# Key scratch in device memory: one copy per slot of a head, two loads per unit instead of six

## The reference, cut to what matters

```python
k = jnp.einsum('btd,dnh->btnh', source_input, wk)        # layer 0; layer 1 is alike
logits = jnp.einsum('btnh,bfnh->bnft', k, q * HEAD_DIM ** (-0.5))
attn = jnp.einsum('bnft,btnh->bfnh', softmax(logits), v)
x = x + jnp.einsum('bfnh,nhd->bfd', attn, wo)
```

## Time and profile before

| | |
|---|---|
| median of 3 runs | 303.28 us |
| the traced execution itself | 301.85 us, span 299.8 us |
| PE, DVE, ACT, POOL busy | 93%, 76%, 69%, 23% of the span |
| granted TensorE clock | full (1.0) throughout |
| DMA | 27.54 MB; HBM read 20.42 MB, written 6.42 MB |
| stores of kparts | 24 of 256 KB |
| loads of kpair | 186: 62 each of 96, 64 and 32 KB |

### The profile page before, as it was taken

How to read it: one execution, slowest core, us unless ns; L and a number is a source line. 1 busy time by engine, 2 the same in 40 slices (tenths; PEclk the granted TensorE clock), 3 DMA queues, 4 the chain that set the end, 5 groups by cost and what they waited for, 6 DMA issues and landing times.

```text
span 299.8 us, 10438 instructions
## 1 busy us (share of the span) xinstructions
PE 278.4 (93%) x4414; PEld 178.8 (60%) x4418; DVE 226.8 (76%) x376; ACT 207.3 (69%) x427; POOL 68.9 (23%) x139
## 2 busy tenths in 40 slices
PE   7989899989899989889999999999889988899995
PEld 6445567656666655453656577676556655436675
DVE  5877699989799982474478999998899860744583
ACT  7864789988778978622444889999788976234350
POOL 5603475101111012510022874101010210110001
PEclk9999999999999999999999999999999999999999
DMA  7954515532222470233200026422222100000000
GB/s 249 415 203 119 157 56 174 179 119 85 63 58 81 110 275 0 107 132 104 83 1 2 3 83 223 149 81 81 61 78 65 46 2 2 2 0 2 0 2 22
DMA packets 10737, 27.54 MB, mean 92 GB/s; under 512 B 2193, under 2 KB 3313, under 8 KB 10306
## 3 DMA queue, kind: packets, MB, share of 16 engines
q1 hardware_dynamic: 10640, 26.83, 27.1%
q10 hardware_dynamic: 50, 0.03, 0.0%
HBM read 20.42 MB, written 6.42 MB: 90 GB/s over the span
## 4 chain that ended last, share of the span: by engine, by line
PE 63%; DVE 13%; SPq 7%; DMA 6%; ACT 5%; issue 4%; POOL 1%; DVEq 0%; POOLq 0%
PE bank L1160 61%; SPq L306 6%; DVE mx L913 6%; DMA kpair<-k_scratch 4%; ACT probs L605 3%; DMA ctxT_s<-in_ctxT 2%; DVE o_rec L869 1%; DVE v_all L860 1%; DVE s_neg L969 1%; DVE xn L836 1%; DVE st L817 1%; PE bank L1497 1%; PE bank L1541 0%; ACT kpair L740 0%; SPq L329 0%
## 5 line engine op out<-in xcount | busy, mean ns | idle before, releaser
L913 DVE TENSOR_REDUCE mx<-bank 128x2 f32<-128x1024 f32 x128 | 149.8, 1215 | 9.1 <-PE bank L1160 7.7
L605 ACT ACTIVATE probs<-bank 128x512 f32<-128x512 f32 x256 | 140.7, 597 | 21.4 <-PE bank L1160 17.9
L1160 PE MATMUL bank<-q_exp,kpair 64*128 64x128 bf16 x1024 | 82.4, 218 | 1.1 <-ACT q_exp L528 1.1
L1160 PE MATMUL bank<-probs,v_all 128*9 128x128 f32 x2048 | 79.9, 274 | 2.0 <-ACT probs L605 1.4
L1160 PE MATMUL bank<-kpair,q_rows 64*128 64x512 bf16 x256 | 68.0, 382 | 8.9 <-DVE mx L913 5.4
L1160 PEld LDWEIGHTS bank<-q_exp,kpair 64*128 64x128 bf16 x1024 | 55.1, 94 | 28.9 <-ACT probs L605 14.5
L1160 PEld LDWEIGHTS bank<-probs,v_all 128*9 128x9 f32 x2048 | 43.4, 90 | 18.6 <-ACT probs L605 4.8
L471 POOL CAST m_rows<-negm 128x2 bf16<-128x2 f32 x32 | 6.3, 197 | 131.1 <-DVE negm L920 131.1
L1160 PEld LDWEIGHTS bank<-kpair,q_rows 64*128 64x128 bf16 x256 | 20.9, 93 | 16.3 <-DVE mx L913 8.1
L528 ACT ACTIVATE v_all<-bank 128x512 f32<-128x512 f32 (+1 forms) x20 | 10.6, 536 | 13.7 <-PE bank L1160 13.7
L395 POOL TENSOR_TENSOR y<-ve,mhalf 128x1 f32<-128x1 f32 (+1 forms) x10 | 5.8, 580 | 53.1 <-DVE ve L823 53.1
(11 more groups left out here) (230 smaller groups left out, 349.9 us busy)
## 6 DMA issues: line engine op xcount, KB each, us to landing
k_scratch<-kparts SPq DMA_DIRECT2D x24, 256.0 KB, 3.3
kpair<-k_scratch SPq DMA_DIRECT2D x62, 96.0 KB
kpair<-k_scratch SPq DMA_DIRECT2D x62, 64.0 KB
ctxT_s<-in_ctxT SPq DMA_DIRECT2D x4, 512.0 KB, 9.0
mask_s<-in_mask SPq DMA_DIRECT2D x2, 1024.0 KB, 9.6
kpair<-k_scratch SPq DMA_DIRECT2D x62, 32.0 KB
wM<-in_packM SPq DMA_DIRECT2D x1, 1728.0 KB, 7.0
wB<-in_packB SPq DMA_DIRECT2D x1, 654.0 KB, 6.4
```

What stands on the lines that cost most here:

```text
L605: act.activation(probs[:, j % 4, :], slot_bank(l, "b", n, j), ACT.Exp).then_inc(S("slot_free"), 1)
L913: V.tensor_reduce(mx[n % 2][:, w, :], bank[:, 2 * (w % 2):2 * (w % 2) + 2, :], AX.X, ALU.max) \
L1160: return T.matmul(out_, lhsT=lhsT, rhs=rhs, start=start, stop=stop, **kw)
```

## The change

The scratch tensor holds the 6 slots of every head in place of the 3 parts. A store writes a key part into each of its slots in one transfer (source repeated); a load takes a whole head, 48 rows of 4 KB, in one transfer. The tables that place queries and first keys follow the new row order, slot first and dimension second.

```diff
-K_LOADS = 2 * PARTS
+K_LOADS = 2
+STORES = 2 * PARTS
-kscr = nc.dram_tensor("k_scratch", (2, B, PARTS, H, HD, SK), BF16, kind="Internal").ap()
+kscr = nc.dram_tensor("k_scratch", (2, B, len(SLOTS), H, HD, SK), BF16, kind="Internal").ap()
 def load_head(eng, l, p, b, u, a):
-    for kp in range(PARTS):
-        times = K_TIMES[kp]
-        row = a * HOFF + K_BASE[kp]
-        src = kscr[l, b, kp, p * 2 + a:p * 2 + a + 1, :, :].rearrange("h d t -> (h d) t")
-        src = src.unsqueeze(1).to_broadcast([HD, times, SK])
-        eng.dma_start(kpair[u][row:row + times * HD, :], src).then_inc(S(f"k_loaded{u}"), 16)
+    src = kscr[l, b, :, p * 2 + a, :, :]
+    eng.dma_start(kpair[u][a * HOFF:a * HOFF + HR, :], src).then_inc(S(f"k_loaded{u}"), 16)
 # store_k
     for kp in range(PARTS):
-        sp.dma_start(kscr[l, b, kp, :, :, t:t + SK // 2],
-                     kparts[:, kp, b * SK + t:b * SK + t + SK // 2]).then_inc(S(f"k_stored{b}"), 16)
+        first = K_BASE[kp] // HD
+        dst = kscr[l, b, first:first + K_TIMES[kp], :, :, t:t + SK // 2].rearrange("s h d t -> (h d) s t")
+        src = kparts[:, kp, b * SK + t:b * SK + t + SK // 2].unsqueeze(1)
+        sp.dma_start(dst, src.to_broadcast([P, K_TIMES[kp], SK // 2])).then_inc(S(f"k_stored{b}"), 16)
 # constants(): selq and selk
-    (h % 2) * HOFF + K_BASE[kp] + d * K_TIMES[kp] + qp
+    (h % 2) * HOFF + K_BASE[kp] + qp * HD + d
```

More of the change, by code:

```diff
@@ L337, in cross_k @@
                 if n % NP == (l == 0 and n < NP):
-                    sp.wait_ge(S(f"k_stored{n // NP}"), 16 * 2 * PARTS * (l + 1))
+                    sp.wait_ge(S(f"k_stored{n // NP}"), 16 * STORES * (l + 1))
                 if l or n >= U:
@@ L449, in split_k @@
                 if l and i == 0:
-                    pool.wait_ge(S("k_stored1"), 16 * 2 * PARTS)
+                    pool.wait_ge(S("k_stored1"), 16 * STORES)
                 pool.tensor_copy(kparts[:, 0, cols], s_sb[:, i, :]).then_inc(S("k_pool"), 1)
@@ L532, in prep_k @@
                 if l and c == 0:
-                    act.wait_ge(S("k_stored0"), 16 * 2 * PARTS)
+                    act.wait_ge(S("k_stored0"), 16 * STORES)
                 copy(kparts[:, 0, c * 512:(c + 1) * 512], bank[:, k_bank(l, c), :]).then_inc(S("k_high"), 1)
@@ L1735, in constants @@
             for d in range(HD):
-                selq[h * HD + d, h // 2 % 2, qp, (h % 2) * HOFF + K_BASE[kp] + d * K_TIMES[kp] + qp] = one
+                selq[h * HD + d, h // 2 % 2, qp, (h % 2) * HOFF + K_BASE[kp] + qp * HD + d] = one
     selk = np.zeros((4 * HD, PARTS, P), np.uint16)
@@ L1740, in constants @@
             for d in range(HD):
-                selk[h * HD + d, kp, h * HOFF + K_BASE[kp] + d * K_TIMES[kp] + qp] = one
+                selk[h * HD + d, kp, h * HOFF + K_BASE[kp] + qp * HD + d] = one
     kone = np.array([[float(r % HOFF >= HR)] for r in range(P)], np.float32)
```

## The result

The changed kernel took 311.44 us in the median (309.30 to 312.31, 4 runs) where the kernel before took 303.01 on the same chip (300.60 to 303.51, 4 runs): a ratio of 1.0284, with an interval of 1.0207 to 1.0361. It is slower, as forecast, but by about 8.4 us where 1.4 were forecast, and the time lies outside the range. Run again later, against a kernel before of 301.54, it gave 1.027 (1.021 to 1.033). The traced execution took 311.05 us, span 309.2 against 299.8: 9.4 us to be found.

The account below looks back on a forecast made before the run. PE, busy 93%, bounds it, with key loads late in a few units. Start +1.7, units 6 to 8 -1.2, layer 1 -0.3 +1.1 -0.3, odd late transfers +0.4: +1.4, 304.7 us; own range 303.7 to 306.0, 8 in 10 301.7 to 306.4.

Parts of the forecast that it names:

- Unit 23's forecast wait of 0.8: Layer 1: load 23 lands at 193.95, needed at 193.15; new stall 0.8, with slower pace after it +1.1 us.
- unit 26: Layer 1, no store near: load path of 3.97 + 2.25 becomes 4.6, its stall goes, -0.3 us.
- the load then becomes shorter: 4.6: At the start, SyncE's first load takes 4.6 us from first issue to landing, before 5.75; unit 1 stalls, +1.7 us.
- no shorter load: Upper bound on the start's cost, 2.8 us in place of +1.7, if the first load does not get shorter.
- in time by 0.7: Layer 0: load 6 lands at 54.75, needed at 55.46, so unit 6 does not wait.
- 6 and 8 are freed: Stalls of units 6 and 8 go (0.4 + 0.7), unit 7 gives 0.1: -1.2 us of 2.32.
- Unit 22: Layer 1: load 22 lands at 187.45, needed about 188.0, so its stall goes, -0.3 us.
- Eight or more engines: Rival: loads run on eight or more engines, no stall at units 7 and 23; -1.9, about 301.5 us; chance 0.16.
- No queueing: Rival: loads do not queue behind stores, stalls at units 7 and 23 fall away; -1.3, 302.0 us; chance 0.13.
- The start hides it: Rival: ScalarE and GpSimd get ahead during unit 1's 1.7 us, units 0 to 3 give it back; 303.0 us; chance 0.09.
- Costlier stores: Rival: three-dimensional or scattered stores could run at half rate; +7 at full size, +3.5 at a quarter, 306.8 us; chance 0.12.
- That issues get no shorter: Case set aside without a chance: six issues become two, so no shorter issue was ruled out.

Follow-up runs that it names:

- the held-back store: Changed kernel, with the second half of batch 1's stores in layer 0 issued only once load 6 has landed; 318.68 us, one execution.

## Why the prediction was right in sign and wrong in size

**Right.** Loads run on six engines (152 to 154 GB/s, forecast 154). The first load goes out at 24.08 (24.6). Issues are of 0.69 us (0.67). Written bytes 12.71 MB (12.7). The queue is in order on an engine (the held-back store). The start, unit 7 and unit 23 stall. Unit 23's forecast wait of 0.8 was hidden in the first trace, where PE was slow at half clock, and is there, with 1.18, in the second. That unit 26 gave -0.27 (-0.3) is partly luck: its wait is gone, but its load path went from 6.77 us to 6.50 and not to 4.6, and it landed 0.05 us before its use.

**At the start: "the load then becomes shorter: 4.6".** This is the step that failed. From first issue to landing it took 6.30 us (24.08 to 30.38) where the forecast had it fall from 5.75 to 4.6. That is no disturbance: loads of the changed kernel with nothing beside them take 5.6 to 6.5. The sum of first bytes at +1.4, 2.55 of bytes and 0.65 left out that a load reaches its rate late. DMA share in tenths, 94 to 100 us in slices of 0.15, of a load that was issued at 94.67 with nothing beside it:

```profile
DMA  0000000000000092700123342423444343572000
```

The first rows move 1.45 us after the issue, then there is a gap, and the steady 0.4 begins at about 2.5 us. The bytes take 3.6 us, from 96.1 to 99.7, for which 2.55 had been reckoned, and the load lands at 100.53, 0.8 later: 5.86 in place of 4.6. It is not a matter of six engines: the same sum gives 3.97 and 3.03 us for eight and sixteen, where loads alone took 4.6 to 5.3 and 3.6 to 4.2. The start cost 2.9 in place of 1.7 (the load went out 0.5 earlier than forecast and took 1.7 longer), just over the bound of 2.8 that I had named "no shorter load".

**Units 6 and 7: "in time by 0.7" and "6 and 8 are freed".** Load 5 went out 4.55 us later than before (48.18 for 43.63), just as PE was 4.56 late, so the forecast's chain can be shifted as a whole: landing at 59.3, needed at 60.0. It landed at 62.03, 2.7 later. Two sizes account for most of it, measured where the second store was held back: 0.9 because the engines get going 2.3 us after the issue and not 1.4, and some 1.6 for six engines that need 10.7 us for what was reckoned as 9.05. I had taken the bytes of every transfer at the rate of its best stretch with no gap between one and the next. Units 6 to 8 gave +1.3 in place of -1.2. **Unit 22**, the same pattern, gave +1.5 for -0.3.

**Not in the forecast at all:** the clock, +1.65 in the first trace, behind unit 1's wait; the second fall cost nothing that load 23 had not cost already. The trace of before has a full clock throughout, and I priced waits as if it would stay so. What the falls cost in the median is less certain: the second trace of the same kernel has one in another place, and filling one wait gained nothing. And unit 15, +0.6 net of what came back: I looked for transfers ahead of the loads and for none behind.

Term by term against the forecast: start +1.2, units 6 to 8 +2.5, unit 22 +1.8, unit 23 +0.3 (1.44 for 1.1), clock +1.65, unit 15 +0.6, the rest -0.1: 8.0, the distance between +1.4 and +9.4. The mechanism was the forecast's, but for the clock and unit 15; what fell was the landing time of a load, and with it the sign at units 6 and 22, which had been reckoned in time by 0.7 us or less.

**The rivals.** *Eight or more engines* was built: at eight it is 1.015, slower, not the 301.5 us of that rival, as the same mis-sized landing would have it (the sum of this rival takes 3.97 us for what took 4.6 to 5.3); at sixteen it is no difference to before. *No queueing*: refuted by the held-back store. *The start hides it*: the delay of 4.55 us at unit 2 was still whole at unit 5. *Costlier stores*: a half moved at 339 GB/s while a load was in flight with it and the first load went out as forecast, so no half-rate stores; yet this rival's 306.8 came nearest, by luck. *That issues get no shorter* was rightly left out.

**Open.** Why the bytes of a load start with a gap; why `wM` slows an earlier load by about 2 us, and a store right behind a load by less; where the clock falls, since it differs between executions of one kernel and did so without a wait for keys ahead of it.

## What to carry to other kernels

Before you trade several transfers for one, write down the outermost dimension of the new one: a source with 6, 8 and 48 rows outermost ran on 6, 8 and 16 engines and gave 1.028, 1.015 and 0.998 for the same bytes. Bytes moved from reads that are repeated to writes that are repeated cost nothing only where the reads behind them have slack; store what the first consumer needs first, and issue its load before the rest of the stores (0.992). When a margin in a forecast is below the error of one transfer's latency (here 0.7 against 1 to 2.7 us), it is no margin: price the late case.

## What the runs showed of the hardware that was not expected

- A load of two transfers, 48 rows of 4 KB each, reached its steady rate on six engines some 2.5 us after its issue, though its first rows moved after 1.45; landing took 4.9 to 5.8 us from the last issue on six engines, 4.0 to 4.6 on eight, 3.3 to 3.9 on sixteen.
- Issues with three dimensions took 0.69 us, those of 48 contiguous rows mostly 0.30 to 0.42.
- A transfer issued 0.7 us behind a load slowed it by 1.9 to 2.3 us (6.7 to 7.2 against 4.9).
- While a load ran beside a store, its six engines fell behind their rate: 291 GB/s over all sixteen from 55 to 56 us, against 398 for stores alone.
- After waits of 2.77 and 1.66 us PE ran at a granted clock of 0.50 (in the stretches 31.0 to 33.6 and 198.0 to 201.0). The first cost 1.65 us; the second cost nothing more, since the next load landed no sooner than PE came to it. Work put into one such wait removed the fall there and gained nothing in the median.
